# Five batches of a graph layer's first pass from count strips in SBUF instead of gathered rows

## What is computed

```python
edge_index = jnp.stack([src, dst])
h = jnp.maximum(_layernorm(x, axis=-1), 0.0)
# first layer: one of two linear maps by edge type, summed at the destination
Xs = h[src]
m_data = Xs @ W_data.T + b_data
m_ctrl = Xs @ W_control.T + b_control
msg = jnp.where((edge_types == 0)[:, None], m_data, m_ctrl)
agg = jax.ops.segment_sum(msg, dst, num_segments=n)
x = x + relu(agg + (h @ W_self.T + b_self))
# second layer: two hops
h = jnp.maximum(_layernorm(x, axis=-1), 0.0)
norm = deg_inv_sqrt[row] * deg_inv_sqrt[col]
z = out = h
for _ in range(2):
    z = jax.ops.segment_sum(z[row] * norm[:, None], col, num_segments=n)
    out = out + z
x = x + out / 3
```

## Time and profile before

| | us |
|---|---|
| median of 3 runs (3950.95 to 3958.83) | 3953.74 |
| the profiled execution | 3954.94 |
| its span | 3952.7 |
| PE busy (share of the span) | 3401.3 (86%) |
| POOL busy | 2739.2 (69%) |
| ACT busy | 2121.5 (54%) |
| DVE busy | 1925.3 (49%) |

### The profile page before, as it was taken

The page is one execution under the profiler, slowest core; times in us unless marked ns, Lnnn a source line. Parts: engine busy times, 40 slices in busy tenths (PEclk is TensorE's granted clock), DMA queues, the critical chain, the costliest instruction groups (busy, mean ns, idle before and its releaser), DMA issues.

```text
span 3952.7 us, 62194 instructions
## 1 busy us (share of the span) xinstructions
PE 3401.3 (86%) x22892; PEld 2748.3 (70%) x22892; DVE 1925.3 (49%) x5238; ACT 2121.5 (54%) x2246; POOL 2739.2 (69%) x2915
## 2 busy tenths in 40 slices
PE   7667778778887878778787899999999799999998
PEld 4344545445554545445454599999999799999998
DVE  7523666667666667666666522333333222222223
ACT  4000233223232323323223488899998699999997
POOL 2677777777777777777777566666666466666666
PEclk9788889889898898889989899999999899999999
DMA  6222343443334334343333577888888978888876
GB/s 195 87 63 64 113 129 112 129 124 116 125 113 130 113 120 132 113 129 113 126 117 113 165 233 232 254 241 248 251 247 276 289 233 236 233 233 232 236 234 200
DMA packets 389431, 676.87 MB, mean 171 GB/s; under 512 B 65350, under 2 KB 313553, under 8 KB 380931
## 3 DMA queue, kind: packets, MB, share of 16 engines
q1 hardware_dynamic: 278563, 409.02, 31.8%
q0 software_dynamic: 109696, 263.44, 24.4%
q10 hardware_dynamic: 864, 0.39, 0.0%
HBM read 510.59 MB, written 162.00 MB: 170 GB/s over the span
## 4 chain that ended last, share of the span: by engine, by line
PE 41%; POOL 40%; issue 13%; DVE 2%; DMA 2%; ACT 1%; SPq 0%; POOLq 0%; DVEq 0%; ACTq 0%
POOL rows L890 40%; PE wide L1188 36%; PE sums_bank L1102 3%; ACT strip_ring L1027 1%; PE wide L1063 1%; DMA stage<-strips 1%; POOL stage L930 0%; DVE big L1232 0%; DVE flat L1272 0%; DMA hop_table<-stage 0%; DVE xin L1420 0%; DVE scaled L1413 0%; DMA big<-in_x 0%; DVE scaled L1422 0%; PE turned_bank L1136 0%
## 5 line engine op out<-in xcount | busy, mean ns | idle before, releaser
L890 POOL DMA_INDIRECT rows<-typed_table,index x1661 | 1589.9, 957 | 506.1 <-issue 505.9
L1027 ACT CAST strip_ring<-stage 128x1792 fp32r<-128x1792 uint8 x896 | 1494.4, 1688 | 137.8 <-PE wide L1188 115.5
L1188 PE MATMUL wide<-table_parts,strip_ring 128*128 128x256 f32 x12544 | 1539.0, 284 | 28.6 <-ACT strip_ring L1027 26.0
L1188 PEld LDWEIGHTS wide<-table_parts,strip_ring 128*128 128x128 f32 x12544 | 1524.5, 193 | 32.2 <-ACT strip_ring L1027 17.1
L890 POOL DMA_INDIRECT rows<-hop_table,index x1162 | 1109.7, 955 | 599.7 <-issue 314.2
L1018 ACT CAST stage<-wide 128x392 uint16<-128x392 f32 x1024 | 497.0, 485 | 1277.9 <-PE wide L1145 1271.6
L1136 PE MATMUL turned_bank<-all_twos 128*128 128x512 bf16 x3328 | 1170.9, 411 | 0.0
L1100 PE MATMUL sums_bank<-rows,hot 128*128 128x129 f32 x3322 | 514.9, 319 | 362.5 <-DMA rows<-typed_table,index 346.1
L1538 DVE TENSOR_SCALAR stage<-counts,stage 128x128 bf16<-128x128 int16 x2048 | 559.6, 335 | 470.2 <-PE wide L1145 469.9
L1100 PEld LDWEIGHTS sums_bank<-rows,hot 128*128 128x128 f32 x3322 | 486.2, 230 | 420.2 <-issue 385.0
L1145 PE MATMUL wide<-stage 128*128 128x196 bf16 x2048 | 687.5, 336 | 99.1 <-DVE stage L1540 99.1
(11 more groups left out here) (147 smaller groups left out, 735.6 us busy)
## 6 DMA issues: line engine op xcount, KB each, us to landing
stage<-strips SPq DMA_DIRECT2D x896, 224.0 KB, 3.8
strips<-stage SPq DMA_DIRECT2D x64, 1568.0 KB
rows<-typed_table,index POOLq DMA_INDIRECT x1661
rows<-hop_table,index POOLq DMA_INDIRECT x1162
resid<-xin SPq DMA_DIRECT2D x50, 256.0 KB, 3.7
xin<-resid SPq DMA_DIRECT2D x50, 256.0 KB, 5.0
typed_table<-flat SPq DMA_DIRECT2D x49, 256.0 KB, 2.1
table_parts<-hop_table SPq DMA_DIRECT2D x14, 896.0 KB, 9.7
```

The source lines that it names most:

```text
L890: pool.indirect_dma_start(out=rows[:, o % RING, c, 0:width_of(k)].bitcast(F32), out_offset=None, in_=tables[k], in_offset=bass.IndirectOff ...
L1027: act.copy(strip_ring[:, number % STRIP_RING], counts_ring[place]).then_inc(strip_cast, 1)
L1188: last = pe.matmul(wide[:, nth % 4, 0:PARTS * P], strip_ring[:, number % STRIP_RING, b - first, :], table_parts[:, b, :, :].rearrange("p n ...
```

## The change

The first-pass sums of five batches (20 tiles, 2560 nodes) are no longer made from gathered rows. For them the kernel makes two count strips per tile, one of all edges and one of the edges of type 0. Both stay in SBUF and are cast in pieces of seven blocks; TensorE multiplies them with h (high and low part) from `table_parts` into 2 x 128 sums per node, VectorE copies these, TensorE multiplies them with the weights (`turn_typed`), and VectorE adds the self part and the biases times the counts.

- Gathering begins with group 41; the first pass has 167 slots instead of 208. The degrees that were a by-product of gathering come from `count_group` for the first 44 groups: ten of them in slot 0, then one per slot.
- Quads and typed steps are spread over slots 5 to 163 by a cost list. `fill` is gone. A quad has three or four wide operations on VectorE instead of five, four of which were narrow.
- In the preparation h goes to HBM as two parts for the first 50 tiles (`h_rows`) and into the upper part of `table_parts` directly for the others; `load_h` fetches the first half before the pass. The self part goes to HBM (`own_rows`) and comes back per batch.
- `table_parts` holds h of the first layer during the typed steps. The finished batches' parts of k = 0 go to HBM only and are reloaded in 14 pieces, as between the hops.
- First-pass sums use one PSUM bank (the other is for typed sums); `sum_group` waits for the addition of the group before. `scaled` has one buffer and `xin` two in this pass.

The diff, cut to its core:

```diff
-FILL = 16
-CELL_START = 24
-CELL_END = 206
-CELL_BATCHES = 3
+TYPED_BATCHES = 5
+TYPED_TILES = TYPED_BATCHES * NODE_BLOCKS
+TYPED_BLOCKS = 7
+TYPED_RING = 2
+WORK_START = 5
+WORK_END = 3
+QUAD_COST, TYPED_QUAD_COST, TYPED_STEP_COST = 1.65, 2.1, 2.05
+CELL_BATCHES = 2
+LOW_LOAD = 10
...
+    typed_pieces = real_blocks // TYPED_BLOCKS
+    typed_steps = TYPED_TILES * typed_pieces
+    work = []
+    for tile in range(DENSE_TILES):
+        typed = tile < TYPED_TILES
+        work += [("quad", tile * QUADS + n, TYPED_QUAD_COST if typed else QUAD_COST) for n in range(QUADS)]
+        work += [("step", tile * typed_pieces + n, TYPED_STEP_COST) for n in range(typed_pieces if typed else 0)]
+    work_cost = sum(cost for _, _, cost in work)
+    work_slots = slots_in[0] - WORK_START - WORK_END
...
+                sp.wait_ge(own_ready, i + 1)
+                sp.dma_start(by_block[:, i * PAIR:(i + 1) * PAIR, :], in_blocks(own_stage[i % OWN_STAGES], PAIR)
+                             ).then_inc(own_stored[i % OWN_STAGES], 16)
+                if (i + 1) * PAIR <= low_blocks:
+                    sp.wait_ge(h_low, i + 1)
+                    sp.dma_start(h_by_block[:, i * PAIR:(i + 1) * PAIR, :],
+                                 h_stage[i % H_STAGES].rearrange("p b n f -> p b (n f)").bitcast(F32)).then_inc(h_stored[i % H_STAGES], 16)
...
+            def low_of_h(first, end):
+                for i in range(first, end):
+                    pool.wait_ge(h_high, i + 1)
+                    parts = h_parts(i)
+                    pool.tensor_tensor(parts[:, :, 1, :], in_blocks(normed[i % 2], PAIR), parts[:, :, 0, :].bitcast(F32), ALU.subtract
+                                       ).then_inc(h_low, 1)
...
+            def high_of_h(i):
+                in_place = (i + 1) * PAIR > low_blocks
+                if not in_place and i >= H_STAGES:
+                    act.wait_ge(h_stored[i % H_STAGES], 16 * (i // H_STAGES))
+                act.wait_ge(h_ready, i + 1)
+                parts = table_parts[:, i * PAIR:(i + 1) * PAIR] if in_place else h_stage[i % H_STAGES]
+                act.copy(parts[:, :, 0, :], in_blocks(normed[i % 2], PAIR)).then_inc(h_high, 1)
...
+                def cast_typed(number):
+                    tile, piece = divmod(number, typed_pieces)
+                    place = number % TYPED_RING
+                    if number >= TYPED_RING:
+                        act.wait_ge(typed_used, number - TYPED_RING + 1)
+                    act.wait_ge(strip_kept, keeps_before[tile + 1])
+                    columns = slice(piece * TYPED_BLOCKS * P, (piece + 1) * TYPED_BLOCKS * P)
+                    act.copy(typed_ring[:, place].rearrange("p n b f -> p n (b f)"), count_bytes[:, :, columns]).then_inc(typed_cast, 1)
...
                     pe.wait_ge(hot_ready, o + 1)
-                    if o >= 2:
+                    if k == 0 and o:
+                        pe.wait_ge(added, o)
+                    elif o >= 2:
                         pe.wait_ge(added, o - 1)
...
+                def typed_step(number):
+                    tile, piece = divmod(number, typed_pieces)
+                    bank = typed_bank[tile % 2]
...
+                    if piece == 0 and tile >= 2:
+                        pe.wait_ge(typed_read, tile - 1)
+                    pe.wait_ge(typed_cast, number + 1)
+                    for b in range(TYPED_BLOCKS):
+                        for n in range(PARTS):
+                            last = pe.matmul(bank[:, agg].rearrange("p (n f) -> p n f", n=TYPES), table_parts[:, piece * TYPED_BLOCKS + b, n, :],
+                                             typed_ring[:, number % TYPED_RING, :, b, :],
+                                             start=(piece == 0 and b == 0 and n == 0),
+                                             stop=(piece == typed_pieces - 1 and b == TYPED_BLOCKS - 1 and n == PARTS - 1))
+                    last.then_inc(typed_used, 1)
...
-                    for w in range(QUAD):
-                        cell = slice(first + w, first + w + 1)
-                        dve.tensor_scalar(quad_low[place][:, w, :], count_up, cell_low[:, cell], cell_weight[:, cell],
-                                          ALU.is_equal, ALU.mult)
-                    dve.tensor_tensor(quad_hot[place], count_quads,
-                                      cell_key[:, first:first + QUAD].unsqueeze(1).to_broadcast([P, hot_columns, QUAD]), ALU.is_equal
-                                      ).then_inc(strip_hot_ready, 1)
+                    low, typed_low = quad_low[place]
+                    dve.tensor_tensor(low, count_quads[:, 0:P, :], by_cell(cell_low, P), ALU.is_equal).then_inc(low_raw, 1)
+                    last = dve.tensor_tensor(quad_hot[place], count_quads, by_cell(cell_key, hot_columns), ALU.is_equal)
+                    dve.wait_ge(low_raw, quad + 1)
+                    if tile < TYPED_TILES:
+                        dve.tensor_tensor(typed_low, low, by_cell(cell_typed, P), ALU.mult)
+                    dve.tensor_tensor(low, low, by_cell(cell_weight, P), ALU.mult).then_inc(strip_hot_ready, 1)
+
+                def make_count_hot(c, half):
+                    if c and half == 0:
+                        dve.wait_ge(count_used, c)
+                    first = c * CHUNKS + half * QUAD
+                    dve.tensor_tensor(count_hot[half], count_quads[:, 0:P, :],
+                                      local[:, first:first + QUAD].unsqueeze(1).to_broadcast([P, P, QUAD]), ALU.is_equal
+                                      ).then_inc(count_hot_ready, 1)
```

More of the change, by code:

```diff
@@ L578, in gnn_kernel @@
         assert all(cells_turn_slot[s] + 1 <= first_quad_slot(s) for s in range(DENSE_BATCHES))
         assert all(slot_of_quad((s - CELL_BATCHES + 1) * NODE_BLOCKS * QUADS - 1) <= cells_turn_slot[s] for s in range(CELL_BATCHES, DENSE_BATCHES))
[L581 to L588 removed]
+        assert max(cells_turn_slot) < slots_in[0]
@@ L1099, in sum_rows @@
                     if k == 0:
-                        last = pe.matmul(sums_bank[:, bank, 0:TILE], hots[:, c, :].bitcast(F32), rows[:, slot, c, 0:TILE].bitcast(F32), **ends)
+                        last = pe.matmul(sums_bank[:, bank, 0:TILE], hots[:, c, :].bitcast(F32), typed_rows[:, slot, c, :], **ends)
                     else:
@@ L1139, in make_cells @@
                 def make_cells(quad):
                     pe.wait_ge(strip_hot_ready, quad + 1)
-                    for w in range(QUAD):
-                        nth, half = divmod(quad * QUAD + w, 2)
-                        if half == 0 and nth >= CELL_BANKS:
+                    place = quad % 2
+                    for nth in range(keeps_through(quad - 1) if quad else 0, keeps_through(quad)):
+                        _, pair, kind = keeps[nth]
+                        if nth >= CELL_BANKS:
```

748 lines of the change are left out of this document (520 added, 228 removed).

## The result

The changed kernel takes 4018.7 us (median of 4 runs, 4014.6 to 4023.1) beside 3953.6 us for the kernel before (4 runs): a ratio of 1.0163, 95% interval 1.0146 to 1.0181. It is 65 us slower, where 181 us faster was forecast, and lies outside the range. The profiled execution took 4016.2 us, its span is 4014.5 us.

The account below looks back on a forecast made before the run. GpSimd's gathers were taken to bound the first pass, TensorE the hops. The last sum, at 2051.6 instead of 2239.2 us, comes 188 us earlier; with 6 us for the transition, 3954.9 - 188 + 6 = 3773 us, range 3640 to 3920.

Parts of the forecast that it names:

- Ten count groups stand in VectorE's slot 0: Start of the first pass: their chain of about 2.1 us each delays the start by 16 us (bounds 3 and 30).
- 2.5 us is everything else: VectorE in the first pass before: 6.7 us busy per slot, 4.2 of them quads, the remainder carried into the plain slot.
- The typed tile of 57 us: First pass, ScalarE and TensorE in turn: 57 us a tile, 11.8 us per slot (bounds 49 and 64 us), 20 tiles.
- the plain slot of 10.9 us: First pass, 62 slots of the other 44 tiles: VectorE's work plus waits, 10.9 us each (bounds 10.06 and 12.2).
- GpSimd's floor: First pass: 1461 operations, all taken as gathers, at 1.258 us each, so 10.06 us per group.
- The preparation: Stage ahead of the first gather: extra stores, cast and subtraction add 28 us (bounds 8 and 45).
- The queues are the larger part: Preparation: 9.6 MB more in the first 25 pairs cost 35 us, less some 10 us of free share.
- The single bank: First-pass sums in one PSUM bank: no cost of its own, as VectorE's 0.52 us addition comes first in each slot.
- Contention: VectorE's bf16 products in SBUF slow GpSimd's gathers by 70 us in all (at most 145), hidden in the forecast.
- Half clock in the typed steps: Rival 3: TensorE stays at half clock in typed steps, 77 us a tile, 4173 us in all; chance 0.08.
- The rival of handoffs: Rival 2: handoffs between four engines cost 1 us more per slot everywhere, 3932 us; chance 0.14.
- GpSimd as the pace: Rival 1: GpSimd still paces the first pass, 159 slots at 10.06 us plus 70 us contention, 3627 us; chance 0.14.

## Why the prediction was wrong

**The step that failed** is "Ten count groups stand in VectorE's slot 0". It priced the chain of hot, narrow products and additions there and stopped; 30 more of them stand in slots 5 to 34, one at the end of each slot, and to these the prediction gave neither work nor wait. Queued behind each of these reads is `add_group`, for which TensorE waits. The prediction had said of this addition that VectorE "does it first in each slot": it does, but the slot begins on VectorE only when the read before it is done. The runs put 109 us on the count reads. The trace of before could not show the wait, but the order of the code did.

**The same reads in the other slots.** Places and turned cells are read in the kernel before too. There VectorE hardly waited for them, as its list of waits shows (107.6 us, 16 times after):

```profile
DVE cell_first L1548 <- PE wide L1158: 4.4, 2, 2.7
```

When the pace went to the loop of VectorE and TensorE, they came onto the path: 97 us with the count reads already put off. "2.5 us is everything else" was a busy time and held no waiting. Together the reads are 206 of the 243 us. With them put off and nothing else changed, the profiled execution (3814.3 us) lies 41 us above the forecast: 24 us in the preparation, 21 in slots 5 to 34, whose count groups still have work of their own, and -4 in all the rest.

**The typed tile of 57 us and the plain slot of 10.9 us** were sized rightly as work: the changed kernel's slots without a read take 11.86 and 10.86 us. With the reads put off, 12.45 and 11.81 us per slot are 60.4 and 57.3 us per tile of 4.85 slots, and the plain slot is 10.73. Loop and bounds held (49 and 64, 10.06 and 12.2). In a typed tile of that kernel two casts of 3.36 us in all and 0.35 us of waiting make 1.86 us a step where 1.83 was forecast, and quads follow each other on VectorE in 1.14 us where 1.16 was.

**GpSimd's floor** was read 1% too low. The 1461 operations of the earlier trace rows are not all gathers: 15 fetch cells. The starts of two sums before lie 10.16 us apart on the mean, not 10.06, and plain slots that GpSimd paces take 10.18 to 10.28 us with three and four batches.

**The preparation** was +28 and is +52.8 us. "The queues are the larger part" is not borne out for h: its bytes hold 3 us, with three places for it. With two places ScalarE waited for its stores to end, which a third place mended without moving a byte less. "GpSimd is free for 92 of 117 us" took the subtraction as hidden, but it stands in ScalarE's loop. The timeline of ScalarE, after, second half:

```profile
142.60 0.88 ACT L1197 ACTIVATE flat<-big 128x128 f32<-128x128 f32 x2 [0.94 <-POOL table_parts L1090]
143.38 0.35 ACT L1220 COPY flat<-sums_bank 128x256 f32<-128x256 f32 x1
143.63 0.40 ACT L1214 CAST table_parts<-flat 128x256 fp32r<-128x256 f32 x1
```

Each pair, ScalarE waits 0.9 us for the subtraction that frees its input: with it a pair takes 2.34 us (142.60 to 144.94) where 1.62 was forecast. The order of ScalarE's work held 10 us of the excess and the places for h 18 us. Of the 24 us that are left over the kernel before, the bytes of h hold 3. The trace points at most of the other 21: with three places the first 24 pairs take 70 us (52 before) and the last 24 take 46 (42 before), and in the first half, whose order had stayed, ScalarE waits for the subtraction. Waits of the first 170 us, three places:

```profile
ACT flat L1197 <- POOL flat L1090: 22.2, 23, 2.6
```

No run took this wait away, so that it holds the 21 us is read, not shown.

**The single bank** "adds no cost of its own": wrong by 0.4 us in each plain slot with the reads put off (16 us of the run's time), right with four batches.

**Contention** was taken at 70 us, hidden. The mean gather is 0.971 us after and was 0.957: 14 ns x 1333 = 19 us of GpSimd's time.

**The start, the transition and the hops**: slot 5 comes 5 us later behind the first gather than forecast, and what follows the last sum takes 4 us more than forecast.

**The rivals.** Half clock in the typed steps (4173 us) had the sign of the result but not its cause: the clock is 0.80 and 0.89 there, not 0.5, the slots without a read take the forecast's time at it, and fillers that raise it cost 169 us. The rival of handoffs had the right kind of cause, 1 us in every slot, 3932 us. It was spread evenly, where the truth is uneven: 4.6 us over the forecast in each of 30 slots, 3.5 of them at one named wait, and some 2.6 us in 25 later slots with a read. GpSimd as the pace (3627 us) did not appear with five batches; it did with three and four.

**The question that was not asked** is how many batches. The sum itself gave the hint: 97 slots at 11.8 us beside a floor of 10.06 say that with five batches GpSimd no longer sets the pace. The "whole possible gain" of 412 us was counted for 41 groups; of the four sizes tried, the one with 33 groups fewer is the fastest.

## What to carry to other kernels

For every wait that a change adds, write down the instruction behind it on the same engine and who waits for that; and do it for each place where the step is repeated, not only for the first. A read of a small result that nobody needs soon belongs behind the work that others wait for: here moving it a few instructions later was worth 206 us. When work is taken from the engine that paces a stage and given to others, compute both paces as a function of how much is moved and stop at the crossing. From there on small waits of the other engines, hidden until now, must be priced too.

## What the runs showed of the hardware that was not expected

The 512-column bf16 products of two SBUF tiles on VectorE (0.415 us each, 672 of them) touch the gathers, but little. Of the changed kernel's 1333 gathers, the 208 that start while such a product runs take 1.047 us on the mean and up to 1.20; the 873 that meet none take 0.961. Over all of them the mean rises from 0.957 to 0.971 us, while one gather beside a longer two-input operation took 1.63 us. Where nothing else paces GpSimd, its operations come 1.269 us apart in the kernel with three batches, within 1% of the 1.258 us before. And the granted clock is by itself a poor sign of time lost: it was 0.91 in plain slots of 12.70 us with fillers, and 0.69 in plain slots of 11.27 us without.
